# A row buffer in memory between the patch embedding and the attention of a fused vision-text block, with a new order of all engines

## What is computed

```python
h = tok(x, ln1_g, ln1_b, W, b, ln2_g, ln2_b)       # patches, layer norm, product, layer norm
h = concatenate([h, txt], axis=1)                  # (64, 273, 256)
h = h + attn(layernorm(h), Wq, bq, Wk, bk, Wv, bv, Wo, bo)
h = h + ffn(layernorm(h), W_r, W_k, W_v, mu_r, mu_k)

# attn: n, s, e = 64, 273, 256; h, d = 16, 16
def proj(W, b):
    y = jnp.einsum('nse,fe->nsf', x, W) + b
    return y.reshape(n, s, h, d).transpose(0, 2, 1, 3)
scores = jnp.einsum('nqhd,nkhd->nhqk', Q, K) * scale
attn = jax.nn.softmax(scores, axis=-1)
out = jnp.einsum('nhql,nlhd->nqhd', attn, V).reshape(n, s, e)
return jnp.einsum('nse,fe->nsf', out, Wo) + bo

def ffn(x, ...):
    x_prev = x shifted by one row
    xr, xk = mu_r * x + (1 - mu_r) * x_prev, mu_k * x + (1 - mu_k) * x_prev
    return sigmoid(xr @ W_r.T) * (square(relu(xk @ W_k.T)) @ W_v.T)
```

## Time and profile before

| what | us |
|---|---|
| median of 3 runs | 1717.25 |
| lowest, highest | 1715.13, 1725.07 |
| the profiled execution's own time | 1719.71 |
| its span | 1718.0 |
| TensorE busy in it | 1442.6 |
| VectorE, ScalarE, POOL busy | 1244.6, 1128.1, 910.5 |

### The profile page before, as it was taken

One profiled execution on the slowest core, in us unless ns is written; L12 is line 12 of the kernel. 1 busy time (PEld: TensorE's weight loads), 2 busy tenths in 40 slices (PEclk: granted clock), 3 DMA queues, 4 the chain that ended last, 5 costly groups with the idle time before them and its releaser, 6 DMA issues. The chain is left out here.

```text
span 1718.0 us, 51431 instructions
## 1 busy us (share of the span) xinstructions
PE 1442.6 (84%) x17678; PEld 1353.0 (79%) x17678; DVE 1244.6 (72%) x3109; ACT 1128.1 (66%) x2410; POOL 910.5 (53%) x1593
## 2 busy tenths in 40 slices
PE   3587898898799888989898898987989879898866
PEld 3577888798788877888887888887888878787755
DVE  5477887787668777868787787776777677786543
ACT  3456686677577677767666776776666667676554
POOL 2231475456555455556564665555544656556356
PEclk8688999899899889999999999998989999998988
DMA  5178687779677778768878887678778587868650
GB/s 132 40 145 144 152 153 117 148 156 142 126 122 149 132 132 147 150 122 146 150 125 152 138 153 152 127 144 136 132 139 137 120 133 132 149 130 125 119 79 28
DMA packets 676232, 225.56 MB, mean 131 GB/s; under 512 B 591051, under 2 KB 647175, under 8 KB 675975
## 3 DMA queue, kind: packets, MB, share of 16 engines
q1 hardware_dynamic: 392615, 186.09, 53.2%
q10 hardware_dynamic: 283360, 36.18, 19.0%
HBM read 119.28 MB, written 90.05 MB: 122 GB/s over the span
## 5 line engine op out<-in xcount | busy, mean ns | idle before, releaser
L1771 PE MATMUL bank<-wqkv,xnT 128*128 128x384 f32 x1656 | 352.5, 359 | 15.8 <-DVE xnT L1571 14.9
L1771 PEld LDWEIGHTS bank<-wqkv,xnT 128*128 128x128 f32 x1656 | 299.1, 200 | 21.5 <-DVE xnT L1571 16.8
L1875 PE MATMUL bank<-wtok,xT 128*126 128x258 f32 (+1 forms) x1800 | 267.8, 308 | 0.0
L1668 ACT ACTIVATE arena<-qk,ymask 128x384 f32<-128x384 f32 x368 | 199.5, 608 | 81.1 <-DMA qk<-qkv_dram 42.7
L1875 PEld LDWEIGHTS bank<-wtok,xT 128*126 128x126 f32 (+1 forms) x1800 | 249.0, 209 | 0.0
L1400 POOL TENSOR_TENSOR mixp<-mixf,mixp 128x384 fp32r<-128x384 f32 x184 | 184.2, 1014 | 86.0 <-ACT mixp L1747 85.9
L1376 POOL TENSOR_TENSOR hb<-hc,bob 128x768 f32<-128x768 f32 x46 | 84.4, 1835 | 190.3 <-DVE h L1594 180.9
L1580 DVE TENSOR_TENSOR qkvt<-bank,bqkv 128x384 f32<-128x384 f32 x276 | 149.7, 546 | 29.2 <-PE bank L1771 28.1
L1689 ACT ACTIVATE xcols<-xim 84x640 f32<-84x640 f32 (+1 forms) x192 | 126.8, 695 | 47.5 <-DVE xs L1506 26.8
L1698 ACT ACTIVATE xT<-bank 128x420 fp32r<-128x420 f32 (+14 forms) x285 | 104.2, 419 | 62.7 <-PE bank L1856 46.4
L1344 POOL TENSOR_TENSOR rs<-ve,small 126x1 f32<-126x1 f32 (+1 forms) x192 | 134.4, 700 | 15.1
(11 more groups left out here) (119 smaller groups left out, 3339.1 us busy)
## 6 DMA issues: line engine op xcount, KB each, us to landing
qkv_dram<-qkvt SPq DMA_DIRECT2D x138, 384.0 KB
xim<-in_x SPq DMA_DIRECT2D x128, 294.0 KB
qk<-qkv_dram ACTq DMA_DIRECT2D x46, 768.0 KB, 10.5
arena<-qkv_dram SPq DMA_DIRECT2D x368, 48.0 KB
out<-h SPq DMA_DIRECT2D x45, 384.0 KB, 3.9
o_dram<-probs SPq DMA_DIRECT2D x108, 96.0 KB, 2.3
on<-o_dram SPq DMA_DIRECT2D x73, 128.0 KB
o_dram<-probs SPq DMA_DIRECT2D x88, 48.0 KB, 2.0
```

What stands on the lines that cost most here:

```text
L1668: kb_sb.done(A.activation(kb[:, :, yy, :].rearrange("p (a u) k -> p a u k", u=UNITS), qk[:, :, HD:2 * HD].rearrange("p (a u) k -> p a u k" ...
L1771: ins = mm(psum, left(a, k), right(b, k), start=t == 0, stop=t == len(terms) - 1)
L1875: ins = mm(place("tok", 0, t)[0:pr, 0:E + 2], xT[:, a, ch, :, :].rearrange("p i w -> p (i w)")[:, r0:r0 + pr], wtok[:, b, ch, :], start=n ...
```

## The change

All rows of `h` now go through `h_dram`, a buffer of 17472 x 256 in memory. A patch tile is stored there in one DMA, or in two where it crosses an image's end (`patch_pieces`), and waits no longer for a slot of `hc`. The text is copied from the input to the buffer by four DMAs of 16 images each, at steps 1, 2, 3 and 7 of the new table, the first three ahead of the first image's load (step 4). A new job `hin` loads a chunk with one DMA (the last chunk, of 192 rows, with two), after `xn_sb` and `hb_sb` of the chunk three before, the stores of its last four tiles and its text; VectorE's first `bn_stats` of a chunk waits for it. `row_pieces` calls `spread` with 16 in place of 9. `bn_stats` at `st2` and `st3` have one more wait each, for the `mv2` and `mv3` of the tile or chunk before. All of `AT` and nearly all of `BANK` have new numbers: 8558 steps where there were 8572. The jobs of the other kinds are the same in number and work. The diff, with the tables cut to their first lines:

```diff
--- before.py
+++ after.py
@@ -32,6 +32,7 @@
 RING = 3 * TROWS
 PAD = TROWS - 1
 OIMAGES = 8
+TIMG = 16
 OSTEP = T * E + 4 * T * HD
...
     load=[
-        [5, 14, 28, 54, 93, 139, 185, 259, 389, 439, 535, 685, 773, 884, 1055, 1193, 1280, 1400, 1589, 1672,
...
+        [4, 14, 28, 54, 93, 125, 183, 230, 313, 342, 380, 519, 635, 818, 968, 1068, 1114, 1302, 1381, 1487,
...
     txt=[
-        [1, 2, 3, 4, 151, 303, 309, 527, 679, 766, 876, 915, 1114, 1240, 1291, 1455, 1651, 1658, 1830, 2027,
...
+        [1, 2, 3, 7],
...
+    hin=[
+        [94, 170, 285, 374, 444, 567, 777, 877, 1132, 1231, 1480, 1628, 1783, 2058, 2120, 2442, 2611, 2725,
...
 
 def patch_pieces(t):
 
-    out = []
-    for a, b in cut(PT * t, PT * t + patch_rows(t), [PATCHES]):
-        shift = (T - PATCHES) * (a // PATCHES)
-        for lo, hi in cut(a + shift, b + shift, [TT]):
-            for at, rows in spread(lo, hi - lo, 32):
-                out.append((at - shift - PT * t, rows) + place_of(at))
-    return out
-
-
-def text_pieces(m):
-    a = T * m + PATCHES
-    return [(at - a, rows) + place_of(at) for lo, hi in cut(a, a + TXT, [TT]) for at, rows in spread(lo, hi - lo, 32)]
+    first = PT * t
+    return [(a - first, b - a, a + (T - PATCHES) * (a // PATCHES))
+            for a, b in cut(first, first + patch_rows(t), [PATCHES])]
 
 
 def row_pieces(c):
 
     return [(at // T, at % T, rows) + place_of(at)[1:]
-            for lo, hi in cut(CT * c, min(CT * c + CT, TOKENS), [TT, T]) for at, rows in spread(lo, hi - lo, 9)]
+            for lo, hi in cut(CT * c, min(CT * c + CT, TOKENS), [TT, T]) for at, rows in spread(lo, hi - lo, 16)]
 
 
...
 PATCH_DMAS = [len(patch_pieces(t)) for t in range(PTILES)]
-TEXT_DMAS = [len(text_pieces(m)) for m in range(IMAGES)]
 ROW_DMAS = [len(row_pieces(c)) for c in range(CHUNKS)]
 HEAD_DMAS = [len(head_pieces(c)) for c in range(CHUNKS)]
 OUT_ROWS = [min(CT, TOKENS - CT * c) for c in range(CHUNKS)]
 OUT_DMAS = [1 if rows == CT else -(-rows // TT) for rows in OUT_ROWS]
+H_DMAS = OUT_DMAS
...
 
 
 def chunk_tiles(c):
-    return [t for t in range(PTILES) if any(piece[2] == c for piece in patch_pieces(t))]
-
-
-def chunk_texts(c):
-    return [m for m in chunk_images(c) if any(piece[2] == c for piece in text_pieces(m))]
+
+    lo, hi = CT * c, CT * c + OUT_ROWS[c]
+    return [t for t in range(PTILES) if any(at < hi and at + rows > lo for first, rows, at in patch_pieces(t))]
 
 
...
 
         qkv_dram = nc.dram_tensor("qkv_dram", (SLOTS, CT, HEADS, QKV), F32, kind="Internal").ap()
+        h_dram = nc.dram_tensor("h_dram", (TOKENS, E), F32, kind="Internal").ap()
         o_dram = nc.dram_tensor("o_dram", ((OIMAGES + 2) * OSTEP,), F32, kind="Internal").ap()
 
...
-        patch_in = Own(ctx, nc, "patch_in", PATCH_DMAS, 4)
-        text_in = Own(ctx, nc, "text_in", TEXT_DMAS, 6)
+        patch_out = Own(ctx, nc, "patch_out", PATCH_DMAS, 4)
+        text_out = Own(ctx, nc, "text_out", 4 * [1], 4)
+        rows_in = Own(ctx, nc, "rows_in", H_DMAS, SLOTS)
 
...
                         load_rest()
-                for m in due(s, "txt", 0):
-                    c = text_pieces(m)[-1][2]
-                    after(xn_sb, c - SLOTS, 3)
-                    after(hb_sb, c - SLOTS, 1)
-                    for t0, rows, cc, i, p in text_pieces(m):
-                        text_in.done(m, sp.dma_start(hc[p:p + rows, cc % SLOTS, i, :],
-                                                     txt[m:m + 1, t0:t0 + rows, :].rearrange("b t e -> (b t) e")))
+                for n in due(s, "txt", 0):
+                    dst = h_dram.rearrange("(b t) e -> b t e", t=T)[TIMG * n:TIMG * n + TIMG, PATCHES:T, :]
+                    text_out.done(n, sp.dma_start(dst, txt[TIMG * n:TIMG * n + TIMG, :, :]))
                 for t in due(s, "hdma", 0):
-                    c = patch_pieces(t)[-1][2]
-                    after(xn_sb, c - SLOTS, 3)
-                    after(hb_sb, c - SLOTS, 1)
                     after(h_sb, t, 1)
-                    for t0, rows, cc, i, p in patch_pieces(t):
-                        patch_in.done(t, sp.dma_start(hc[p:p + rows, cc % SLOTS, i, :], yh[t0:t0 + rows, t % 2, :]))
+                    for first, rows, at in patch_pieces(t):
+                        patch_out.done(t, sp.dma_start(h_dram[at:at + rows, :], yh[first:first + rows, t % 2, :]))
+                for k in due(s, "hin", 0):
+                    after(xn_sb, k - SLOTS, 3)
+                    after(hb_sb, k - SLOTS, 1)
+                    for t in chunk_tiles(k)[-4:]:
+                        after_all(patch_out, t)
+                    after_all(text_out, chunk_images(k)[-1] // TIMG)
+                    if OUT_ROWS[k] == CT:
+                        rows_in.done(k, sp.dma_start(hc[:, k % SLOTS, :, :], h_dram[CT * k:CT * k + CT, :].rearrange("(i t) e -> t i e", t=TT)))
+                    else:
+                        for i in range(H_DMAS[k]):
+                            rows = min(TT, OUT_ROWS[k] - TT * i)
+                            rows_in.done(k, sp.dma_start(hc[0:rows, k % SLOTS, i, :], h_dram[CT * k + TT * i:CT * k + TT * i + rows, :]))
                 for i in range(TILES):
                     for k in due(s, "qkv_out", i):
                         after(qkv_sb, k, 2 * i + 2)
...
                 for t in due(s, "st2", 0):
                     pr = patch_rows(t)
+                    mv2_sb.wait(dve, t - 1, 1)
                     y_sb.wait(dve, t, 1)
                     st2.done(V.bn_stats(bn2[0:pr, :], place("tok", 0, t)[0:pr, 0:E]))
...
-                    patch_in.wait(dve, t - 2)
+                    patch_out.wait(dve, t - 2)
                     h_sb.done(V.scalar_tensor_tensor(out=yh[0:pr, t % 2, :], in0=place("tok", 0, t)[0:pr, 0:E], scalar=rs2[0:pr, :],
                                                      in1=b2b[0:pr, :], op0=ALU.mult, op1=ALU.add))
 
                 for i in range(TILES):
                     for k in due(s, "st3", i):
+                        mv3_sb.wait(dve, k - 1, i + 1)
                         if i == 0:
-                            for t in chunk_tiles(k)[-4:]:
-                                patch_in.wait(dve, t)
-                            for m in chunk_texts(k):
-                                text_in.wait(dve, m)
+                            rows_in.wait(dve, k)
                         st3.done(V.bn_stats(bn3[:, i, :], hc[:, k % SLOTS, i, :]))
                     for k in due(s, "mv3", i):
                         rs3_pool.wait(dve, k - 1, 4)
```

More of the change, by code:

```diff
@@ L753 @@
     x=[
-        [int(b) for b in "2552321142213645101050552147526356413126772342246166511631265562"],
-        [int(b) for b in "5257217054024072645451007062276463430672526647520445312716277734"],
-        [int(b) for b in "2520740415253466401254232330312065724505250556756163006101564437"],
+        [int(b) for b in "2552377375071522761507367163343407264322544272107600136250716305"],
+        [int(b) for b in "5257415465137371227013010111216537376207763416243323503575453625"],
+        [int(b) for b in "2520200214711415361451413031607010155577264204772213273561423400"],
@@ L757 @@
     ],
     tok=[
-        [int(b) for b in "7275103543037140167617051742373761240452567567144101016276114643402743612454277706532570342032450153"],
+        [int(b) for b in "7275162615046752046135057404362545242502057534267245315314363170706557437140712325527106060701350367"],
     ],
     xt=[
-        [int(b) for b in "4660660214702037430432203471300320425277136607"],
-        [int(b) for b in "6776743075061775303005415317634106377355772230"],
+        [int(b) for b in "7333135630503725325226141435114332710701060702"],
@@ L764 @@
+        [int(b) for b in "0476403472750500014063002771262706126564714375"],
     ],
     qkv=[
-        [int(b) for b in "5021162333545656141227552211455064630413414672"],
-        [int(b) for b in "3253641572702410215704465057617321505375075263"],
-        [int(b) for b in "4410744045020362400653362736126525224603107705"],
-        [int(b) for b in "6662001763541040355570653063556351636467714632"],
-        [int(b) for b in "7354663335165511644025016272127726430347127555"],
-        [int(b) for b in "5161542315711633321300327335653071206674072702"],
-    ],
@@ L773 @@
-    s=[
-        [int(b) for b in "2763622266660570623757455700047304431546031267"],
-        [int(b) for b in "6400755743026637030235203066131033751110732732"],
-    ],
-    pt=[
-        [int(b) for b in "5266660016344261616022322107002745632736400613"],
-        [int(b) for b in "7731530405403614602522003613653326450653664106"],
-    ],
-    av=[
-        [int(b) for b in "2162211261037335027360425270725101132066051447"],
-        [int(b) for b in "5205754736224372736461306762101044364231400771"],
+        [int(b) for b in "5231336621216225566550271654451632612076565523"],
@@ new lines @@
+        [int(b) for b in "3775605230722674050430463021536676444461113036"],
+        [int(b) for b in "4616462700006524565770401320374770244270616222"],
```

(61 more changed lines are left out.)

1 line of the change is left out of this document (added), and 1095 rows, old and new, of tables (add, av, carry, d).

## The result

The changed kernel takes 1640.5 us (median of 4 runs, 1632.1 to 1647.0) beside 1721.2 us (1715.1 to 1728.2) for the kernel before on the same chip: ratio 0.953, 95% interval 0.947 to 0.959.

What follows compares the result with a forecast made beforehand. The order of jobs, chiefly TensorE's waits for `on`, was taken to bound the middle. Minus 31, plus 8, plus 3, plus 9, minus 11 took 1719.7 to 1697.7 us, 1695 as median; range 1662 to 1734.

Steps and rivals of the forecast that it cites:

- TensorE's work: Whole kernel: TensorE busy 1442.6 of 1718.0 us, with 275 us in which it stands.
- The middle: 155 to 1590 us: new distances in the step tables shorten TensorE's waits, minus 31, bounds minus 104 and plus 35.
- The term for `on`: First transposes of `on`, in the middle: longer distance gives back 23 us, less standing ahead of the loads 10.
- rival (e): The waits in the middle: over half of the 104 us go, 57 in place of 31, 1669 us; chance 0.10.
- The row buffer's cost: Chunk load ahead of VectorE's `bn_stats`: 17 chunks late by 1.5 us, a third passed on, plus 8; fuller queue plus 3.
- SyncE's saving: SyncE's DMA issues over the kernel: 158 us of issuing less, counting only where an `on` load stands behind it.
- The start: First images: three text DMAs ahead of image 0 make images late, plus 9, bounds 0 and plus 22.
- The tail: Last chunk's chain: 14.7 us of work moves behind its first transposes, minus 11 (0 to minus 15).
- (b): Waits on `on` stay, as SyncE's relief is spent before reaching them: about no change, 1716 us; chance 0.15.
- (d): New order worse in places distances don't show, such as bank turns or `xT` halves: 1732 us; chance 0.09.
- (a): Chunk load late, VectorE stops at L1562 in every chunk: 65 in place of 8, 1752 us; chance 0.12.
- (c): Text block holds the start at its full price, 22 in place of 9: 1708 us; chance 0.08.

Runs made afterwards that it cites:

- The two fillers: Kernel before with 20 small matmuls more per chunk, ahead of TensorE's wait for the rows of `on` (1788.5 us) or behind it (2021.7 us).
- the eight other runs: Profiled executions with the same 17678 matmuls, without the kernels before and after; a line through them rises 0.38 us of work per us at the lower clock level.
- Taking the lead back: Changed kernel with each chunk's load, `bn_stats`, `rstd3` and `xn` up to 90 steps later: 1677.3 us, ratio 0.978.
- taking back a fifth of SyncE's relief: Changed kernel with the tile stores cut into 282 pieces in place of 156: 1657.5 us, ratio 0.965.
- the repeat: The changed kernel measured again with nothing altered, beside the kernel with its text behind images 0 and 1: 1641.7 us, ratio 0.952.

## Why the prediction was right in sign and wrong in size

The forecast missed 55 us: 34 of them in TensorE's work, the rest in its idle time, which fell by 43 us where 22 were forecast.

**TensorE's work was a constant in it.** "So the time is TensorE's work plus 275 us in which it stands": the work was priced at 1442.6 us whatever the waits do. It is 1408.3 after. Every wait of 3 to 5 us was counted once where it costs again in the clock; the earlier trace rows had the sign of it, 0.94 in a middle where TensorE is 88% busy. This is 34 of the 55 us that were missed. The two fillers show the mechanism. That it makes up all of the 34 rests on the line through the eight other runs, which gives 35; no run changes the clock alone.

**The middle, minus 20 predicted (minus 31, plus 8, plus 3), minus 52 of idle time measured.** The term for `on` was 33 (23 of distance, 10 of relief); the wait fell by 70. Its size was rival (e)'s, and its reason was wrong: "0.7 us at the 34 late chunks gives back 23 us" took one link by itself. In the kernel before with some 3 us more of that distance the wait only fell by a third and the time not at all. What the new order does is lengthen all links at once: from the last move of its patch rows to `hc` to its output a chunk spans 215 us of priced work on average instead of 182, so 6.9 chunks are under way instead of 5.8, with the normalisation 12 us further ahead, the heads' store (`o_out`) 76 us behind the transposes instead of 55. Taking the lead back costs some 40 us, and taking back a fifth of SyncE's relief some 20 (predicted for all of it: 10). The two were not tried together, and most of the relief was never taken back, so the gain can't be divided between lead, relief and the longer spacing of the attention jobs, which no run tests by itself. The small terms: sums plus 5 predicted, 17 gained; scores 6 predicted, none gained; both were read from single distances as well. Only the first products came as priced: plus 3, and their wait for `xnT` went from 12.2 to 15.2 (counted from the last transposes of `xn`, that distance is 4.4 and 3.7 in the tables: the term means `xnT`, not `xT`).

**What the buffer has to do with it.** The tables were read for what they change, not for what they presuppose. 87 of the 100 tile stores in the new order stand ahead of the job that frees the slot of `hc` they would have had to wait for; in the old order none. So the buffer lets the patch tiles run ahead of the attention, by 15 us of priced work on average at these tiles, which a ring of three slots forbids. How much the old structure would lose in this order, or whether it would stop for good, wasn't tried.

**The row buffer's cost was right as far as it can be read.** Landing 3.9 predicted, 4.1 measured; 17 chunks late by 1.5 us, 25 late by 1.2 measured (25.5 against 30.9 us of VectorE); DMA share of the middle plus 0.05, 0.78 to 0.84 measured. SyncE's saving was 158, and by the sums of these issues it is 165: a store takes 0.36 us where 0.5 was taken. The third that was passed on to TensorE, plus 8, can't be read from any run.

**The start, plus 9.** Both images came within the bounds (18 to 25: 22.90; up to 12 late: 11.4), but chunk 0 was later by 22 us (17 in the repeat), the far bound. In idle time of TensorE the start is plus 12. And an earlier start is not seen at the end: with the text behind the images the time is 5 us less, if that.

**The tail, minus 11.** It became 14.8 us longer. The term assumed that the last chunk's chain keeps its length while work moves behind it; but an order with more chunks under way stretches every chunk's chain, the last one's too: from its first transposes to its last product a chunk takes 180 us on average instead of 167. The price is paid once, at the end; the gain comes 43 times.

**The rivals.** (b) and (d) didn't happen. (a) happened only in the old order. (c) happened at the start, where chunk 0 came 22 us late, and not at the end. (e) was the right case with 1669: with over half of the 104 us gone (it was 70 us or 67%) and the clock's 34 us on top it would have held.

## What to carry to other kernels

Price a wait of TensorE of several us twice, once as idle time and once as work at half clock behind it (here some 2 us for each fall), and look at the granted clock of a stretch before TensorE's work is called a constant. With engines in a fixed order, compare two orders by how far whole chains are stretched (how many chunks are under way), not by the distance of one link, and ask which buffer permits the stretch. An experiment that takes a part of an effect back prices that part alone, so say how large the part is. A large transfer that is needed late goes behind the first small loads in the queue.

## What the runs showed of the hardware that was not expected

The same 1840 matmuls cost 70 us ahead of a wait and 303 us behind it, with the granted clock at 0.948 and 0.880 over the span. The clock fell at or right behind 27 of the 28 stands of TensorE of 3 us or more in the two middles, and at 7 of the 179 of under 2 us. One program's runs lie 21 us apart (1641.4 and 1662.5), with the clock at 0.947 and 0.938. An issue of a store of up to 126 rows to memory takes SyncE 0.36 us, where a piece from chip memory to chip memory, 44 rows on average, took 0.77. With the same 282 pieces stored to memory the issue takes 0.33, so it is not their size. A copy of 16 x 77 rows from memory to memory takes 0.60.
